# First layer of a graph network kernel: the sums and extrema of an entry made together in one PSUM bank, turned an iteration later and added at once, with a bank for each scan's transposes

## The chip, the cores and the metric

The kernel runs on one core of one Trainium2 chip. The metric is the device time of one execution in microseconds. A core has TensorE (PE, with its weight loads PEld), VectorE (DVE), ScalarE (ACT), GpSimd (POOL) and SyncE (SP), each with an instruction stream of its own; they meet through semaphores. Transfers are issued from SP, ACT and POOL queues and run on 16 DMA engines. TensorE's results go to PSUM, which has eight banks of 128 x 512 f32.

## The reference, cut to what matters

The program is a two-layer graph network over 6250 nodes and 206250 edges (sorted by target `dst`), 128 features. The change touches the first layer's edge stage alone. For each edge

```
z2 = concatenate([node_feat[src], node_feat[dst], edge_feat])
e = relu(z2 @ W_pre + b_pre)
deg = segment_sum(ones, dst)
s = segment_sum(e, dst)
mean_sq = segment_sum(e * e, dst) / safe_deg
mx = segment_max(e, dst)
mn = segment_min(e, dst)
```

that is: a message `e` for each edge, and per target node its count, sum, sum of squares, maximum and minimum. What follows (means, standard deviation, two dense layers, layer norms, a GCN and a GAT layer) is as it was.

## The kernel before, in words

`build` (L100) first makes tables in DRAM: `Atab` and `Btab`, the node features already multiplied by the source part and the target part of `W_pre`; masks `MM` that mark where a target's run of edges begins; and a list of **entries**. An entry is a chunk of 512 edges with a base node; its targets lie in a window of W = 64 nodes from the base. The list has T entries (read from `tb`), and every engine loops over it.

`phase_l0` (L443) is the first layer's edge stage. Each engine runs `pipeline(e, T, U, D, stages)` (L64) with U = 4 and D = 8: in iteration n it performs the listed steps in the written order, each for entry n minus its lag. Nothing else orders the work. `j.at(n)` (L47) is the entry's number plus n, so that `wait(e, s, j.at(-3))` waits until the step that raises `s` has been done for entry j-4, and `j.at(-1)` for entry j-2; `j.slot(4)` is the buffer number modulo 4. The loops are:

- **SyncE** (L513), `(0, loads), (2, load_dst)`. `loads` (L520) reads the entry's chunk and base from `tb`, waits for the gathers of j-4 and issues `ms` (source numbers, L529); waits for `p1` of j-4 and issues `ZR[0:64]` (edge features, 128 KB, L532) and `WB[64:128]` (64 rows of `Btab`, L533); waits for `d1` of j-4 and issues `dstb` (the targets of 512 edges on 64 partitions, 128 KB, L536). `load_dst` (L538) issues `md` (4 KB, L544).
- **GpSimd** (L548): four indirect gathers of `Atab` rows into `G` (L559).
- **VectorE** (L564), `(4, base), (2, d2), (0, d1), (2, hot), (4, d4a), (6, d4b), (4, d3)`. `d1` (L572) turns `dstb` into a one-hot of the target in `ZR[64:128]` (L577). `d2` (L580) adds `Z` and the gathered rows into `EE` (L585). `hot` (L588) makes one-hots `oh` of targets on edges' partitions (L593). `d4a` and `d4b` (L616 to L628) add turned results from the PSUM bank `TT` into `acc` (both at L622). `d3` (L598) runs the two scans, a running maximum and minimum over each target's run (L606, L608).
- **ScalarE** (L632), `(5, a2a), (1, masks), (2, a1), (5, a2b), (2, half), (3, e1), (5, e2)`. `a1` makes relu and square of an entry into `EE` (L639, L641), `half` a bf16 copy of four one-hots (L648), `masks` issues the mask transfer (L656), `a2a` and `a2b` copy the transposed scans from the bank `BK` to `BS` (L663), `e1` and `e2` copy sums (bank `S1`, L675) and extrema (bank `S2`, L681) to SBUF.
- **TensorE** (L685), `(5, p3a), (6, t2), (4, t1), (1, p1), (5, p3b), (3, p2), (5, p4)`. `p1` (L694) multiplies the 128 rows of `ZR` (64 edge features, 64 one-hot rows) with `WB` into `Z` (L702): the edge part plus the target part. `p2` (L706) transposes the relu'd messages into `ET` (L713) and makes sums and sums of squares with the one-hots into `S1` (L720). `t1` (L723) makes the counts (L732) and turns the sums (L733) into `TT`; `t2` (L736) turns the extrema (L740). `p3a` and `p3b` (L742 to L759) transpose the two scans one after the other through the one bank `BK` (L752), the second waiting for ScalarE's copy of the first. `p4` (L761) picks each target's last scan value with one-hots into `S2` (L769). `warm` (L691) is a matmul of zeros that is overwritten; it stands before the first group of `BK`, `Z` and `ET`.

All eight PSUM banks are in use (`Z` 2, `ET` 2, `S1`, `S2`, `BK`, `TT`). Slots before: `ms`, `md`, `ZR`, `WB`, `dstb`, `mm2`, `G`, `oh` four, `EE`, `ohb`, `ST`, `BS` two.

## Time and profile before

| | |
|---|---|
| median of 3 runs | 5884.95 us (5878.37 to 5885.05) |
| the profiled execution | 5883.57 us, its span 5881.6 us |
| mean granted TensorE clock | 0.95 of full |
| PE, DVE, POOL, ACT busy over the span | 92%, 82%, 67%, 48% |
| first layer's edge stage | from about 135 us to 2260 us |
| transfers over the span | 544.72 MB, mean 93 GB/s |

Busy shares are a mean over stages with different limits, so the stage is read by itself: a window gives busy time by engine, a group of lines the mean of one instruction, the waits what ended an engine's idle time, and the timeline the order of starts. Matmuls are pipelined and their ends are modelled, so distances from start to start are surer than durations on PE. A row "L622 ... x2" in a timeline is two instructions merged.

### The profile page before, as it was taken

What the parts mean: (1) busy time and instruction counts of PE and PEld (TensorE: products, weight loads), DVE (VectorE), ACT (ScalarE), POOL (GpSimd) and SP (SyncE); (2) the same over time, 40 slices, a digit from 0 to 9 for tenths busy, and PEclk for the clock granted to TensorE, in tenths of its full rate; (3) what the DMA queues carried; (4) which work ended last, traced back from release to release, by engine and by line L of the source; (5) the groups of instructions that cost most, each with busy time, mean ns of one, the idle gap of its engine ahead of it and who ended that gap; (6) DMA issues with size and microseconds to landing.
All of it is one profiled execution on the core that took longest, in us unless ns stands there. A gap on an engine that the chain in (4) does not pass through costs nothing. (4 is left out here: it accounts for less than half of the span.)

```text
span 5881.6 us, 179579 instructions
## 1 busy us (share of the span) xinstructions
PE 5388.7 (92%) x43454; PEld 4199.9 (71%) x44114; DVE 4796.1 (82%) x12693; ACT 2838.9 (48%) x6715; POOL 3926.1 (67%) x3976
## 2 busy tenths in 40 slices
PE   3999999999999997778888858999999999999993
PEld 3888888888888885457777735666666666666663
DVE  4999999999999996777777667777777777777777
ACT  1566666666666663133333244444444444444445
POOL 2777777777777772067777707777777777777762
PEclk7999999999999998878989869999999999999996
DMA  6666666666666663322222212222222222222221
GB/s 155 161 159 158 158 157 158 157 158 157 158 156 158 157 157 95 91 54 54 53 54 54 52 27 53 52 52 51 50 51 51 51 51 50 51 50 51 51 45 47
DMA packets 667245, 544.72 MB, mean 93 GB/s; under 512 B 365794, under 2 KB 544171, under 8 KB 666853
## 3 DMA queue, kind: packets, MB, share of 16 engines
q0 software_dynamic: 126336, 262.13, 18.9%
q1 hardware_dynamic: 415050, 163.69, 12.1%
q10 hardware_dynamic: 125724, 117.57, 7.7%
q14 instruction: 108, 0.88, 0.1%
q8 instruction: 27, 0.44, 0.0%
HBM read 517.22 MB, written 25.61 MB: 92 GB/s over the span
## 5 line engine op out<-in xcount | busy, mean ns | idle before, releaser
L1766 POOL DMA_INDIRECT Gt<-TAB,metat x1632 | 1631.9, 1000 | 705.9 <-issue 538.8
L559 POOL DMA_INDIRECT G<-Atab,ms x1616 | 1580.3, 978 | 572.3 <-issue 469.4
L1256 POOL DMA_INDIRECT Gc<-XS,metac x672 | 647.5, 964 | 240.1 <-issue 188.4
L1912 ACT COPY P<-PT 128x512 f32<-128x512 f32 x408 | 238.7, 585 | 805.7 <-PE PT L1956 739.0
L663 ACT COPY BS<-BK 128x512 f32<-128x512 f32 x808 | 465.6, 576 | 198.7 <-PE BK L752 190.4
L1401 ACT COPY acc<-CP 128x300 f32<-128x300 f32 x630 | 269.5, 428 | 557.2 <-PE CP L1439 552.3
L606 DVE TENSOR_TENSOR_SCAN ST<-mm,ST,ET 128x512 f32<-128x512 bf16 x404 | 516.7, 1279 | 0.2
L608 DVE TENSOR_TENSOR_SCAN ST<-mm,ST,ET 128x512 f32<-128x512 bf16 x404 | 506.9, 1255 | 0.0
L702 PE MATMUL Z<-WB,ZR 128*128 128x128 f32 x3232 | 429.3, 276 | 68.0 <-DVE ZR L577 67.7
L752 PE MATMUL BK<-ident,ST 128*128 128x128 f32 x3232 | 485.2, 273 | 2.4 <-ACT BS L663 1.8
L1970 PE MATMUL SR<-P,Gt 128*128 128x128 f32 x3264 | 472.8, 288 | 0.0
L1970 PEld LDWEIGHTS SR<-P,Gt 128*128 128x128 f32 x3264 | 395.0, 191 | 70.0 <-issue 70.0
L720 PE MATMUL S<-EE,oh 128*64 128x128 f32 x6464 | 442.2, 279 | 0.0
L1838 DVE TENSOR_TENSOR ln<-acc,LT 1x128 f32<-1x128 f32 x408 | 112.4, 275 | 400.5 <-PE LT L1940 385.9
L702 PEld LDWEIGHTS Z<-WB,ZR 128*128 128x128 f32 x3232 | 428.5, 193 | 11.9
L1414 PE MATMUL OT<-acc 128*128 128x180 f32 x2100 | 429.9, 331 | 0.5 <-ACT acc L1401 0.5
L769 PE MATMUL S<-BS,oh 128*64 128x128 f32 x6464 | 421.7, 273 | 1.4 <-issue 1.4
L639 ACT ACTIVATE EE<-EE 128x512 f32<-128x512 f32 x404 | 255.0, 631 | 347.2 <-issue 273.0
L1923 PE MATMUL SR<-zm,zw 128*128 128x512 bf16 x1531 | 413.6, 380 | 6.5 <-ACT P L1912 1.2
L752 PEld LDWEIGHTS BK<-ident,ST 128*128 128x128 f32 x3232 | 392.6, 141 | 32.8 <-issue 2.5
L1327 DVE TENSOR_SCALAR O<-iotaD,VA 128x300 bf16<-128x300 f16 x1260 | 400.9, 322 | 1.2
L720 PEld LDWEIGHTS S<-EE,oh 128*64 128x64 f32 x6464 | 344.7, 137 | 67.7 <-issue 67.7
(291 smaller groups left out, 12145.1 us busy)
## 6 DMA issues: line engine op xcount, KB each, us to landing
mm<-MM ACTq DMA_DIRECT2D x404, 256.0 KB
ZR<-in_eft SPq DMA_DIRECT2D x404, 128.0 KB
dstb<-DF SPq DMA_DIRECT2D x404, 128.0 KB
Gt<-TAB,metat POOLq DMA_INDIRECT x1632
G<-Atab,ms POOLq DMA_INDIRECT x1616
ad<-ADT SPq DMA_DIRECT2D x816, 0.2 KB
WB<-Btab SPq DMA_DIRECT2D x404, 32.0 KB
Gc<-XS,metac POOLq DMA_INDIRECT x672
```

The costliest lines, as they stand in the source:

```text
L559: e.indirect_dma_start(G[:, k, s, :], None, Atab, bass.IndirectOffsetOnAxis(ap=ms[:, k, s:s + 1], axis=0)).then_inc(l_g[k], 16)
L606: e.tensor_tensor_scan(ST[:, q, 0, :], mm2[:, k, 0, :], ET[q][:, :], ST[:, 1 - q, 0, CH - 1:CH], ALU.mult, ALU.max)
L608: e.tensor_tensor_scan(ST[:, q, 1, :], mm2[:, k, 1, :], ET[q][:, :], ST[:, 1 - q, 1, CH - 1:CH], ALU.max, ALU.min).then_inc(s_d3, 1)
L663: e.copy(BS[:, q, a, :], BK[:, :]).then_inc(s_a2[a], 1)
L702: mm = e.matmul(Z[q][:, s * 128:(s + 1) * 128], ZR[:, k, s * 128:(s + 1) * 128], WB[:, k, :], start=True, stop=True)
L720: mm = e.matmul(S1[a * 64:(a + 1) * 64, 0:128], oh[:, k, s, :], EE[:, q, a, s * 128:(s + 1) * 128], start=(s == 0), stop=(s == 3))
L752: mm = e.transpose(BK[:, s * 128:(s + 1) * 128], ST[:, q, a, s * 128:(s + 1) * 128], ident[:, :])
L769: mm = e.matmul(S2[a * 64:(a + 1) * 64, 0:128], oh[:, k, 4 + s, :], BS[:, q, a, s * 128:(s + 1) * 128], start=(s == 0), stop=(s == 3))
L1256: e.indirect_dma_start(G[:, k, s, :], None, XS, bass.IndirectOffsetOnAxis(ap=meta[:, k, s:s + 1], axis=0)).then_inc(l_g[k], 16)
L1414: mm = e.matmul(OT[k][:, 0:DB], acc[:, 0, h * 128:(h + 1) * 128], C[k][:, h, :], start=(h == 0), stop=(h == NB - 1))
L1766: e.indirect_dma_start(G[:, k, s, :], None, TAB, bass.IndirectOffsetOnAxis(ap=meta[:, k, s:s + 1], axis=0)).then_inc(l_g[k], 16)
L1970: m = e.matmul(SR[q][:, 0:2 * W], G[:, k, s, 0:128], P[:, q, s * 128:(s + 1) * 128], start=(s == 0), stop=(s == 3))
```

## The change

- The sums (`S1`) are no longer made in `p2` but in `p4`, beside the extrema, into one bank `S` (columns 0 to 127 and 128 to 255), and ScalarE copies both at once (`sums`) into `SN` of 256 columns.
- `t1` and `t2` become one step `across`, lag 6: counts, then both turns, into five adjacent parts of `TT`; `d4a` and `d4b` become one add `d4` of 5 x 64 columns, lag 7.
- The bank set free makes `BK` two banks, one for each scan. `p3a` and `p3b` now stand together and each waits only for the copy of its own bank an entry earlier.
- `EE` and `ohb` get four slots instead of two, so `d2` waits for `p4` of j-4 instead of `p2` of j-2.
- `WB` and `dstb` get two slots instead of four. `loads` waits for `p1` of j-2 before `ZR` and `WB`; `dstb` is issued by a step of its own, `load_col`, after a wait for `d1` of j-2.
- The tile of zeros `zm` goes; `warm` streams the 128 columns of `zw` four times.
- The orders on TensorE and ScalarE change as the diff shows.

The diff, without declarations of semaphores and unchanged lines:

```diff
-        WB = sbt(ph, "WB", [128, 4, 128])
-        dstb = sbt(ph, "dstb", [128, 4, CH])
+        WB = sbt(ph, "WB", [128, 2, 128])
+        dstb = sbt(ph, "dstb", [128, 2, CH])
-        EE = sbt(ph, "EE", [128, 2, 2, CH])
+        EE = sbt(ph, "EE", [128, 4, 2, CH])
-        ohb = sbt(ph, "ohb", [128, 2, 4, W], BF16)
+        ohb = sbt(ph, "ohb", [128, 4, 4, W], BF16)
-        S1 = pst(ph, "S1", [128, 512])
-        S2 = pst(ph, "S2", [128, 512])
-        BK = pst(ph, "BK", [128, CH])
+        S = pst(ph, "S", [128, 512])
+        BK = [pst(ph, f"BK{a}", [128, CH]) for a in range(2)]
...
             def loads(j):
-                gathered, done = 64 * j.uses(4, -1), j.at(-3)
+                gathered = 64 * j.uses(4, -1)
                 if not j.first(4):
                     wait_sync(e, l_g[k], gathered, s_sync)
                 e.dma_start(ms[:, k, :], src[0]).then_inc(l_ms[k], 16)
-                if not j.first(4):
-                    wait_sync(e, s_p1, done, s_sync)
+                if not j.first(2):
+                    wait_sync(e, s_p1, j.at(-1), s_sync)
                 e.dma_start(ZR[0:64, k, :], src[1]).then_inc(l_in[k], 16)
-                e.dma_start(WB[64:128, k, :], src[2]).then_inc(l_in[k], 16)
-                if not j.first(4):
-                    wait_sync(e, s_zr, done, s_sync)
-                e.dma_start(dstb[64:128, k, :], src[3]).then_inc(l_db[k], 16)
+                e.dma_start(WB[64:128, j.slot(2), :], src[2]).then_inc(l_in[k], 16)
+
+            def load_col(j):
+                k = j.slot(2)
+                c = e.snap(regs[j.slot(4)], min_val=0, max_val=NCH - 1)
+                if not j.first(2):
+                    wait_sync(e, s_zr, j.at(-1), s_sync)
+                e.dma_start(dstb[64:128, k, :], DF[ds(c * CH, CH)].partition_broadcast(64)).then_inc(l_db[k], 16)
...
-            pipeline(e, T, U, D, [(0, loads), (2, load_dst)])
+            pipeline(e, T, U, D, [(0, loads), (0, load_col), (2, load_dst)])
...
             def d2(j):
                 wait(e, s_p1, j.at(1))
                 wait(e, l_g[j.slot(4)], 64 * j.uses(4))
-                if not j.first(2):
-                    wait(e, s_p2, j.at(-1))
+                if not j.first(4):
+                    wait(e, s_p4, j.at(-3))
...
             def hot(j):
                     wait(e, s_p4, j.at(-3))
+                    wait(e, s_a1, j.at(-3))
...
-            def d4(j, S, n, lo, s_in, s_out):
+            def d4(j):
                 b = kept(e, regs, j)
-                wait(e, s_in, j.at(1))
+                wait(e, s_t, j.at(1))
                 if not j.first(1):
-                    wait(e, s_out, j.at())
-                a = acc[:, lo:lo + n, ds(b, W)]
-                e.tensor_tensor(a, a, S, ALU.add).then_inc(s_out, 1)
+                    wait(e, s_d4, j.at())
+                a = acc[:, 0:5, ds(b, W)]
+                e.tensor_tensor(a, a, TT[:, 0:5 * W].rearrange("p (a n) -> p a n", a=5), ALU.add).then_inc(s_d4, 1)
-            pipeline(e, T, U, D, [(4, base), (2, d2), (0, d1), (2, hot), (4, d4a), (6, d4b), (4, d3)])
+            pipeline(e, T, U, D, [(4, base), (2, d2), (0, d1), (2, hot), (7, d4), (4, d3)])
...
+            def sums(j):
                 wait(e, s_p4, j.at(1))
                 if not j.first(1):
-                    wait(e, s_t2, j.at())
-                e.copy(SN2[:, :], S2[:, 0:128]).then_inc(s_e2, 1)
-            pipeline(e, T, U, D, [(5, a2a), (1, masks), (2, a1), (5, a2b), (2, half), (3, e1), (5, e2)])
+                    wait(e, s_t, j.at())
+                e.copy(SN[:, :], S[:, 0:256]).then_inc(s_e, 1)
+            pipeline(e, T, U, D, [(5, a2a), (5, a2b), (2, a1), (1, masks), (3, half), (5, sums)])
...
             def warm(bank):
-                e.matmul(bank[:, :], zw[:, :], zm[:, :], start=True, stop=True)
+                e.matmul(bank[:, :], zw[:, :], zw[:, :].unsqueeze(1).to_broadcast([128, 4, 128]), start=True, stop=True)
...
+            def across(j):
+                wait(e, s_a1, j.at(1))
+                wait(e, s_e, j.at(1))
                 if not j.first(1):
-                    wait(e, s_e1, j.at())
+                    wait(e, s_d4, j.at())
                 for s in range(4):
-                    for a in range(2):
-                        mm = e.matmul(S1[a * 64:(a + 1) * 64, 0:128], oh[:, k, s, :], EE[:, q, a, s * 128:(s + 1) * 128],
-                                      start=(s == 0), stop=(s == 3))
-                mm.then_inc(s_p2, 1)
+                    e.matmul(TT[:, 2 * W:3 * W], onesb[:, :], ohb[:, j.slot(4), s, :], start=(s == 0), stop=(s == 3))
+                e.transpose(TT[:, 0:2 * W], SN[:, 0:128], ident[:, :])
+                e.transpose(TT[:, 3 * W:5 * W], SN[:, 128:256], ident[:, :]).then_inc(s_t, 1)
...
             def p3(j, a):
                 wait(e, s_d3, j.at(1))
-                if a == 1:
-                    wait(e, s_a2[0], j.at(1))
-                elif not j.first(1):
-                    wait(e, s_a2[1], j.at())
+                if not j.first(1):
+                    wait(e, s_a2[a], j.at())
...
             def p4(j):
+                wait(e, s_oh, j.at(1))
                 for a in range(2):
                     wait(e, s_a2[a], j.at(1))
                 if not j.first(1):
-                    wait(e, s_e2, j.at())
+                    wait(e, s_e, j.at())
                 for s in range(4):
                     for a in range(2):
-                        mm = e.matmul(S2[a * 64:(a + 1) * 64, 0:128], oh[:, k, 4 + s, :], BS[:, q, a, s * 128:(s + 1) * 128],
+                        e.matmul(S[a * 64:(a + 1) * 64, 0:128], oh[:, k, s, :], EE[:, k, a, s * 128:(s + 1) * 128],
+                                 start=(s == 0), stop=(s == 3))
+                for s in range(4):
+                    for a in range(2):
+                        mm = e.matmul(S[a * 64:(a + 1) * 64, 128:256], oh[:, k, 4 + s, :], BS[:, q, a, s * 128:(s + 1) * 128],
                                       start=(s == 0), stop=(s == 3))
                 mm.then_inc(s_p4, 1)
-            pipeline(e, T, U, D, [(5, p3a), (6, t2), (4, t1), (1, p1), (5, p3b), (3, p2), (5, p4)])
+            pipeline(e, T, U, D, [(5, p3a), (5, p3b), (1, p1), (3, p2), (6, across), (5, p4)])
```

## Rows read from the trace of the kernel before

**Rows 1.** The page, costliest groups: out<-in xcount, busy us, mean ns, idle before

```profile
L606 DVE TENSOR_TENSOR_SCAN ST<-mm,ST,ET 128x512 f32<-128x512 bf16 x404 | 516.7, 1279 | 0.2
```

**Rows 2.** Windows of the first layer: busy us per engine (count), granted clock, DMA share, GB/s

```profile
1000.00:2200.00 1200.00, 1188.11 (x13721) 1067.12 (x13949) 1135.81 (x1601) 721.62 (x1601) 889.15 (x913) 1.00 0.62 157
```

**Rows 3.** Groups of lines, 300 to 2150 us, columns as in group 1

```profile
L559 POOL DMA_INDIRECT G<-Atab,ms x1415 | 1383.8, 978 | 467.4 <-issue 410.4 <-DMA ms<-in_meta 43.9 <-DVE EE L585 13.1
L606 DVE TENSOR_TENSOR_SCAN ST<-mm,ST,ET 128x512 f32<-128x512 bf16 x353 | 451.5, 1279 | 0.2
```

**Rows 4.** Waits of VectorE, 404 to 2200 us: us in total, times, longest us

```profile
DVE EE L585 <- PE S L720: 31.6, 135, 0.5
```

**Rows 5.** Timeline of all engines, 1500 to 1511 us: start us, us, engine, line

```profile
1501.12 0.39 PE L692 MATMUL BK<-zm,zw 128*128 128x512 bf16 x1
...
1501.15 0.55 DVE L577 TENSOR_SCALAR ZR<-dstb,baseF,nid 64x512 f32<-64x512 f32 x1
...
1501.78 0.27 PE L740 MATMUL TT<-ident,SN 128*128 128x128 f32 x1
...
1502.20 0.39 PE L692 MATMUL Z<-zm,zw 128*128 128x512 bf16 x1
...
1502.43 1.05 PE L702 MATMUL Z<-WB,ZR 128*128 128x128 f32 x8
1502.45 0.58 DVE L622 TENSOR_TENSOR acc<-acc,TT 128x192 f32 x2
...
1504.22 1.25 DVE L608 TENSOR_TENSOR_SCAN ST<-mm,ST,ET 128x512 f32<-128x512 bf16 x1
1504.33 0.52 SPq L532 DMA_DIRECT2D ZR<-in_eft  x1
...
1504.50 1.09 PE L720 MATMUL S<-EE,oh 128*64 128x128 f32 x16
...
1505.71 0.47 SPq L536 DMA_DIRECT2D dstb<-DF  x1
...
1506.40 0.39 PE L692 MATMUL BK<-zm,zw 128*128 128x512 bf16 x1
```

**Rows 6.** Timeline, 1496.9 to 1499.2 us, where SyncE waited for the matmuls of p1

```profile
1497.14 1.06 PE L702 MATMUL Z<-WB,ZR 128*128 128x128 f32 x8
...
1498.43 0.50 SPq L532 DMA_DIRECT2D ZR<-in_eft  x1
```

**Rows 7.** Timeline of the stage's start, 140 to 165 us

```profile
139.69 0.54 SPq L536 DMA_DIRECT2D dstb<-DF  x1
139.88 1.91 PE L702 MATMUL Z<-WB,ZR 128*128 128x128 f32 x8
...
142.87 0.55 DVE L577 TENSOR_SCALAR ZR<-dstb,baseF,nid 64x512 f32<-64x512 f32 x1 [2.73 <-DMA dstb<-DF]
...
144.55 0.54 SPq L536 DMA_DIRECT2D dstb<-DF  x1
...
148.16 0.55 DVE L577 TENSOR_SCALAR ZR<-dstb,baseF,nid 64x512 f32<-64x512 f32 x1 [1.74 <-DMA dstb<-DF]
...
149.12 0.47 SPq L536 DMA_DIRECT2D dstb<-DF  x1
...
152.14 0.69 DVE L577 TENSOR_SCALAR ZR<-dstb,baseF,nid 64x512 f32<-64x512 f32 x1 [1.09 <-DMA dstb<-DF]
...
154.98 1.25 DVE L608 TENSOR_TENSOR_SCAN ST<-mm,ST,ET 128x512 f32<-128x512 bf16 x1
...
156.29 0.10 PEld L692 LDWEIGHTS BK<-zm,zw 128*128 128x128 bf16 x1 [0.87 <-DVE ST L608]
...
158.11 0.47 SPq L536 DMA_DIRECT2D dstb<-DF  x1
...
162.71 0.55 DVE L577 TENSOR_SCALAR ZR<-dstb,baseF,nid 64x512 f32<-64x512 f32 x1 [1.24 <-DMA dstb<-DF]
```

**Rows 8.** Window of the GCN stage, columns as in group 2

```profile
2500.00:3300.00 800.00, 685.40 (x4283) 569.85 (x4284) 586.88 (x2712) 255.59 (x600) 594.54 (x617) 0.87 0.22 54
```

More of the change, by code:

```diff
@@ L482, in phase_l0 @@
         l_in = [sem(f"l_in{k}") for k in range(4)]
-        l_db = [sem(f"l_db{k}") for k in range(4)]
+        l_db = [sem(f"l_db{k}") for k in range(2)]
         l_m = [sem(f"l_m{k}") for k in range(4)]
@@ L513, in _ @@
         def _(e):
-            for k in range(4):
+            for k in range(2):
                 e.dma_start(WB[0:64, k, :], d["wpre"][256:320, :]).then_inc(l_we, 16)
@@ L573, in d1 @@
                 k = j.slot(4)
-                wait(e, l_db[k], 16 * j.uses(4))
+                wait(e, l_db[j.slot(2)], 16 * j.uses(2))
                 if not j.first(4):
                     wait(e, s_p1, j.at(-3))
-                e.tensor_scalar(ZR[64:128, k, :], dstb[64:128, k, :], baseF[64:128, ds(j.at(), 1)], nid[64:128, 0:1],
+                e.tensor_scalar(ZR[64:128, k, :], dstb[64:128, j.slot(2), :], baseF[64:128, ds(j.at(), 1)], nid[64:128, 0:1],
                                 ALU.subtract, ALU.is_equal).then_inc(s_zr, 1)
@@ L643, in half @@
             def half(j):
-                q = j.slot(2)
+                q = j.slot(4)
                 wait(e, s_oh, j.at(1))
-                if not j.first(2):
-                    wait(e, s_t1, j.at(-1))
+                if not j.first(4):
+                    wait(e, s_t, j.at(-3))
                 e.copy(ohb[:, q, :, :], oh[:, j.slot(4), 0:4, :]).then_inc(s_a1, 1)
@@ L662, in back @@
                     wait(e, s_p4, j.at(-1))
-                e.copy(BS[:, q, a, :], BK[:, :]).then_inc(s_a2[a], 1)
+                e.copy(BS[:, q, a, :], BK[a][:, :]).then_inc(s_a2[a], 1)
             def a2a(j):
@@ L669, in a2b @@
                 back(j, 1)
[L671 to L677 removed]
+            def sums(j):
                 wait(e, s_p4, j.at(1))
                 if not j.first(1):
[L680 to L683 removed]
+                    wait(e, s_t, j.at())
+                e.copy(SN[:, :], S[:, 0:256]).then_inc(s_e, 1)
+            pipeline(e, T, U, D, [(5, a2a), (5, a2b), (2, a1), (1, masks), (3, half), (5, sums)])
         @blk.tensor
         def _(e):
[L687 to L688 removed]
+            e.wait_ge(l_we, 32)
+            e.wait_ge(s_i, 2)
             T = load_T(e, tb, 0)
             def warm(bank):
[L692 removed]
+                e.matmul(bank[:, :], zw[:, :], zw[:, :].unsqueeze(1).to_broadcast([128, 4, 128]), start=True, stop=True)
             def p1(j):
@@ L701, in p1 @@
                 for s in range(4):
-                    mm = e.matmul(Z[q][:, s * 128:(s + 1) * 128], ZR[:, k, s * 128:(s + 1) * 128], WB[:, k, :],
+                    mm = e.matmul(Z[q][:, s * 128:(s + 1) * 128], ZR[:, k, s * 128:(s + 1) * 128], WB[:, j.slot(2), :],
                                   start=True, stop=True)
@@ L712, in p2 @@
                 for s in range(4):
[L713 removed]
+                    mm = e.transpose(ET[q][:, s * 128:(s + 1) * 128], EE[:, j.slot(4), 0, s * 128:(s + 1) * 128], ident[:, :])
                 mm.then_inc(s_p2t, 1)
[L715 removed]
+            def across(j):
+                wait(e, s_a1, j.at(1))
+                wait(e, s_e, j.at(1))
                 if not j.first(1):
[L717 removed]
+                    wait(e, s_d4, j.at())
                 for s in range(4):
[L719 to L740 removed]
+                    e.matmul(TT[:, 2 * W:3 * W], onesb[:, :], ohb[:, j.slot(4), s, :], start=(s == 0), stop=(s == 3))
+                e.transpose(TT[:, 0:2 * W], SN[:, 0:128], ident[:, :])
+                e.transpose(TT[:, 3 * W:5 * W], SN[:, 128:256], ident[:, :]).then_inc(s_t, 1)
             def p3(j, a):
```

61 lines of the change are left out of this document (11 added, 50 removed).

## The prediction

> **What bounds the kernel now.** I read the page first, to find the stage the diff touches: the first layer handles 404 entries, one scan pair each [rows 1]. Windows inside that stage say which engine is full. TensorE is busy 99% of the time at its full granted clock, which is the 2.4 GHz level, VectorE 95%, and the transfers hold 62% of the DMA engines [rows 2]. The groups of lines over 1850 us give the pace: 353 scans, so one entry every 5.24 us, and GpSimd's four gathers at 0.98 us with 0.29 us of issue between them need 5.1 us of it [rows 3]. Then the waits. TensorE has none in the stage. VectorE waits for TensorE's sums of an entry two before, because `EE` has two slots: 31.6 us over 1796 us, or 0.09 us an entry [rows 4]. SyncE holds back `ZR` until the matmuls of `p1` end, and is let go at once [rows 6]. So TensorE's own sequence bounds, and VectorE, GpSimd and SyncE stand within about 5% of it. Such a kernel has little to win from a shorter wait and much to lose from a longer one.
>
> **The loop that the change closes.** Every engine runs its steps in the written order, and in iteration n a step with lag L works on entry n-L. `loads` now waits for `s_p1` at `j.at(-1)`, so the transfers for entry n are issued after the matmuls `p1(n-2)`, where before it was `p1(n-4)`. This follows from `WB` and `dstb` having two slots. `ZR` keeps four but stands behind the same wait, and `dstb` is issued third. In VectorE's iteration n stand `d2(n-2)`, `d1(n)`, `hot(n-2)`, the add, and the scans `d3(n-4)`. In TensorE's iteration n+1 stand first `p3a(n-4)` and `p3b(n-4)`, which wait for those scans, and then `p1(n)`. So `p1(n-2)` releases `dstb(n)`, that releases `d1(n)`, the scans behind `d1(n)` release TensorE, and `p1(n)` ends the loop. It advances two entries, so twice the period is at least its length:
> - From the start of `d1` to the end of the second scan: 1501.15 to 1504.22 + 1.25 = 1505.47, which is 4.32 us [rows 5]. The two adds in it, 0.58 us together [rows 5], become one over the same 320 columns. It lies between 0.29 us, half the pair, and 0.58 us; I take 0.52 us, near the pair, because the columns stay and only one start is saved: 4.26 us.
> - From the scan's end to TensorE: where TensorE waited for a scan it began at 156.29, the scan having ended at 154.98 + 1.25 = 156.23: 0.06 us [rows 7].
> - From the warming matmul of `BK` to the end of `p1`: 1501.12 to 1502.43 + 1.05 = 1503.48, 2.36 us. In it the turns of the sums (1501.78 to 1502.20, 0.42 us) give way to `p3b`'s four transposes. Four transposes with a warming matmul took 1501.12 to 1501.78, 0.66 us, and a warming matmul alone 0.23 us (1502.20 to 1502.43), so `p3b` takes 0.43 us [rows 5]: 2.37 us.
> - From the end of `p1` to the issue of `ZR` where SyncE waited for it: 1497.14 + 1.06 = 1498.20 to 1498.43, 0.23 us [rows 6].
> - From there to the issue of `dstb`: 1504.33 to 1505.71, 1.38 us, `WB` standing between [rows 5].
> - From that issue until `d1` runs. In the steady stage no row shows it, since `d1` never waits there. The nearest rows are those at the start of the stage, where it did: 139.69 to 142.87, 144.55 to 148.16, 149.12 to 152.14 and 158.11 to 162.71, so 3.18, 3.61, 3.02 and 4.60 us [rows 7]. I take their mean, 3.60 us, because the last one was issued among nearly the full traffic and the others among less, and keep 3.02 and 4.60 us as ends.
>
> All but the last is 4.26 + 0.06 + 2.37 + 0.23 + 1.38 = 8.30 us. With 3.60 us the loop is 11.90 us, the period 5.95 us. That is 0.71 us above 5.24 us, and 404 times it 287 us. Against the profiled execution's 5883.6 us this gives 6171 us; the median of the runs lies 1.4 us higher, which makes 6172 us. The ends give periods of 5.66 and 6.45 us, hence 6053 and 6372 us.
>
> The rule nearest to this: the Trainium skill, DMA: Bandwidth & Descriptors, section on the anatomy of one DMA, puts a transfer at about 2.0 us fixed plus bytes over 436 GB/s. An estimate from that page for the 128 KB of `dstb` is 2.3 us, with which the period would be 5.30 us and the time about 5908 us. None of the four rows is that short; what such a landing would do is rival 2.
>
> **The other parts.**
> - SyncE's own work: with nothing to wait for it issued `dstb` at 144.55 and 149.12, 4.57 us apart [rows 7]. Even with another 0.4 us of waits passed and loop turns it keeps 1.0 us of the 5.95 us free, so it stands ready when `p1` ends. Queued behind its longer wait are `md`, issued next after `dstb` and needed by `hot` right behind `d1`, and `ms` for the next gathers. `md` is 4 KB against 128 KB, so I cost it at nothing; if it landed last it could put up to 0.3 us into the loop, inside the ends above. GpSimd needs 5.1 us of 5.95 us and its rows of an entry are wanted two iterations later, so a later `ms` costs nothing while the period is above 5.1 us.
> - Single turn and single add: `across(n-6)` needs the add of entry n-7, which VectorE makes behind the late `d1(n)`. That path is d1's start to the add's end 1.82 us, 0.06 us, the six matmuls 0.4 us, then both groups of sums until the next iteration (1504.50 to 1506.40, 1.90 us [rows 5]): 4.2 us, against 4.32 us by the scans. It is the next limit, 0.1 us behind, and costs nothing of its own. In the profile TensorE's idle time may be shown half before `across`.
> - Sums made two iterations later, `EE` and `ohb` in four slots: VectorE's wait for them (0.09 us) goes. It is not a saving, since `d1` is what comes last now.
> - `BK` in two banks: `p3b` no longer waits for ScalarE's copy. TensorE had no such wait, so nothing. The same copies, one 256-column copy for two of 128, leave ScalarE near the 60% it shows now [rows 2].
> - The warming matmul reads one block four times in place of `zm`. The plain one costs 0.39 us (0.23 us to the next start) [rows 5]. I take the same; were it twice as slow, the two of them in the loop would add 0.46 us, 0.23 us a period, 93 us in all. Less than now is excluded, as the columns streamed are the same.
> - One lag more (7) lengthens the end by part of one iteration, under 3 us: nothing beside the sum.
>
> **The rivals.**
> 1. The transfer lands early enough, and TensorE still bounds. It decides at 2 x 5.24 - 8.30, a landing of 2.2 us. Then the order counts: turns and row counts made at once save part of the 0.42 us [rows 5], by perhaps 0.09 us an entry, and VectorE's slack no longer matters: 404 x 0.09 = 36 us, so 5848 us, **faster**. For it: 99% busy [rows 2], and that transfers started with a lighter load. Against: the shortest landing seen is 0.8 us too long. 7%.
> 2. The landing is shorter than any row shows, between 2.2 and 2.4 us, and the loop just touches TensorE's pace. The period is then 5.25 to 5.35 us, and if the reorder gives nothing back the time is 5888 to 5928 us. For it: the landings at the start spread over 1.6 us, so they hang on what else is moving, and a slower stage moves less. Against: the shortest of the four is 3.02 us, and three of them came while fewer transfers moved than in the steady stage. 6%, of which 4% within 0.2% and 2% above. This is the case of the page's figure named above.
> 3. The clock falls too. TensorE would be idle 0.75 us of 5.95 us. The GCN stage shows what can come with gaps: 685 us busy of 800 us at a granted 0.87 [rows 8], which is 26% of the time at the 1.2 GHz level. There `p1` took 1.91 us [rows 7] against 1.05 us [rows 5], so a TensorE iteration of 5.2 us becomes 9.5 us. With 26% of the time at it the period is 1 / (0.74 / 5.95 + 0.26 / 9.5) = 6.6 us, and the time about 6430 us. For it: `p3a`, `p3b` and their warming matmul now stand together, a long stretch of transposes. Against: the gap is short, and the same three warming matmuls stay in each iteration. 7%. The Trainium skill, TensorE: Matmul & The Clock Gate, Part 4 on transposes, says that transposes do not count as busy in the way matmuls do, which speaks for this case; no row here separates it.
>
> **How the numbers follow.** The loop as costed has 80%, so 6172 us. Its ends are 6053 and 6372 us; I round them outward to 6050 and 6380 us. That leaves out the first two rivals (13%) and the clock case (7%). A measurement can tell this kernel from no change by about 0.2%, 12 us. Slower: 80 + 7 + 2 = 89%; within 0.2%: 4%; faster: 7%.
>
> **What would show it.** Right: a period near 5.95 us; `d1` waiting about 1 us in each entry for the `dstb` transfer; TensorE about 87% busy in the stage, idle before `BK`'s warming matmul or before the row counts; SyncE waiting long for `p1`; VectorE's wait for the sums gone; the later stages unchanged. Wrong: no DMA wait at `d1` and TensorE still 99% busy (rival 1 or 2), or a granted clock under 1.0 (rival 3). A wait of `hot` on `md`, or of the gathers on `ms`, would mean that the loop was closed at another place.

## The result and the profile after

The kernel after takes 6742.1 us (median of 3 runs, 6720.04 to 6742.46) against 5884.95 us: 1.145 times as long, interval 1.1411 to 1.1485. The forecast was 6172 us, with a range to 6380 us: the direction was right, the size was not, and the time lies above the range.

Three quarters of the loss, 637.7 of 859 us, are in the first layer, where the forecast put all of the loss; the rest is where it put nothing. First the page of the kernel after; q14 is the queue that brings the engines their instructions:

```profile
q14 instruction: 361, 2.96, 0.1%
...
L554 POOL DMA_INDIRECT G<-Atab,ms x1616 | 1547.0, 957 | 1250.6 <-DMA ms<-in_meta 781.6
...
L571 DVE TENSOR_SCALAR ZR<-dstb,baseF,nid 64x512 f32<-64x512 f32 x404 | 225.6, 558 | 539.0 <-DMA dstb<-DF 527.7
...
L601 DVE TENSOR_TENSOR_SCAN ST<-mm,ST,ET 128x512 f32<-128x512 bf16 x404 | 514.5, 1274 | 0.0
```

`d1` (L571) stood idle 527.7 us for `dstb`, 1.3 us an entry, which the forecast named as the sign of its loop. The last line answers to [rows 1]. q14 moved 361 packets of instructions; the page of the kernel before has 108 there, which becomes the key to the second part of the loss.

How long the first layer is, from the first to the last start of a scan, in the view of one source line (minimum, median and maximum in ns, then those two starts in us), before and after:

```profile
L606 DVE TENSOR_TENSOR_SCAN ST<-mm,ST,ET x404: 1267/1279/1282, 153.8 to 2268.4; 128x512 f32<-128x512 bf16 x135
```

```profile
L601 DVE TENSOR_TENSOR_SCAN ST<-mm,ST,ET x404: 1267/1273/1278, 152.3 to 2904.6; 128x512 f32<-128x512 bf16 x135
```

2114.6 us became 2752.3 us, that is 5.25 us an entry became 6.83 us (403 steps): 637.7 us. From the last scan to the end of the span 3613.2 us (5881.6 - 2268.4) became 3836.0 us (6740.6 - 2904.6): 222.8 us in stages whose code the change doesn't touch.

Windows of the kernel after, of the scan of L601 alone (us, busy us, times, granted clock, DMA share, GB/s), and the whole row of one of them:

```profile
404.00:1000.00 596.00, 115.19 (x91) 0.96 0.49 126
1000.00:2200.00 1200.00, 225.79 (x178) 0.93 0.47 122
2200.00:2850.00 650.00, 110.79 (x88) 0.87 0.44 110
```

```profile
1000.00:2200.00 1200.00, 1011.32 (x10803) 886.44 (x10803) 842.80 (x1063) 532.68 (x1062) 678.12 (x710) 0.93 0.47 122
```

Against [rows 2] TensorE is busy 84% instead of 99%, and the clock is no longer 1.00 throughout: a granted 0.93 is about 14% of the time at the 1.2 GHz level. An entry takes 596 / 91 = 6.55 us at a granted 0.96, 1200 / 178 = 6.74 us at 0.93, and 650 / 88 = 7.39 us at 0.87. The pace falls with the clock, but it is far above 5.24 us even where the clock is nearly full.

The waits of the kernel after, 300 to 2150 us (us in total, times, longest):

```profile
POOL G L554 <- DMA ms<-in_meta: 467.5, 150, 5.2
DVE ZR L571 <- DMA dstb<-DF: 327.5, 165, 4.8
...
PE TT L705 <- DVE acc L617: 276.4, 146, 4.6
```

And a timeline of two entries at full clock, every step of the forecast loop in it:

```profile
1501.29 0.39 PE L675 MATMUL BK<-zw 128*128 128x512 bf16 x1
...
1502.61 1.05 PE L685 MATMUL Z<-WB,ZR 128*128 128x128 f32 x8
...
1503.89 0.48 SPq L523 DMA_DIRECT2D ZR<-in_eft  x1
...
1505.43 0.40 SPq L531 DMA_DIRECT2D dstb<-DF  x1
...
1506.51 0.39 PE L675 MATMUL BK<-zw 128*128 128x512 bf16 x1
...
1510.08 0.55 DVE L571 TENSOR_SCALAR ZR<-dstb,baseF,nid 64x512 f32<-64x512 f32 x1 [2.69 <-DMA dstb<-DF]
...
1511.73 1.27 DVE L601 TENSOR_TENSOR_SCAN ST<-mm,ST,ET 128x512 f32<-128x512 bf16 x1
...
1511.96 0.28 PE L705 MATMUL TT<-ohb,onesb 128*128 128x64 bf16 x4 [2.43 <-DVE acc L617]
...
1512.92 1.25 DVE L603 TENSOR_TENSOR_SCAN ST<-mm,ST,ET 128x512 f32<-128x512 bf16 x1
...
1514.32 0.39 PE L675 MATMUL BK<-zw 128*128 128x512 bf16 x1
...
1515.64 1.05 PE L685 MATMUL Z<-WB,ZR 128*128 128x128 f32 x8
```

The steps follow one another as predicted: `p1` ends at 1502.61 + 1.05 = 1503.66; `ZR` is issued 0.23 us later, `dstb` 1.54 us after it; `d1` runs 4.65 us after that issue, having stood idle 2.69 us for it; its scans end at 1514.17, TensorE restarts 0.15 us later and ends `p1` at 1516.69. That is 13.03 us for two entries, in one short turn (1501.29 to 1506.51, 5.22 us) and one long (7.81 us). TensorE's idle time is shown before `across`, at L705, as the forecast said it might be.

One thing about the runs below: in some jobs the kernel before itself took 7820 to 7870 us instead of 5885 us, all runs of the job alike, so every ratio there is to the kernel before of the same job.

### The profile page after: what moved, and what is told of

Read it like the earlier page. It is cut to its first block and busy times, and to the rows that moved or that the text cites. A ratio compares the mean times of both kernels' runs of the same rounds, so it can differ in the third digit from the quotient of the medians.

```text
span 6740.6 us, 178054 instructions
## 1 busy us (share of the span) xinstructions
PE 5686.3 (84%) x43859; PEld 4377.8 (65%) x44114; DVE 4711.0 (70%) x12288; ACT 2782.4 (41%) x6311; POOL 3880.2 (58%) x3976
## 5 line engine op out<-in xcount | busy, mean ns | idle before, releaser
L571 DVE TENSOR_SCALAR ZR<-dstb,baseF,nid 64x512 f32<-64x512 f32 x404 | 225.6, 558 | 539.0 <-DMA dstb<-DF 527.7
L664 ACT COPY SN<-S 128x256 f32<-128x256 f32 x404 | 150.4, 372 | 1080.1 <-PE S L739 1019.6
L735 PE MATMUL S<-EE,oh 128*64 128x128 f32 x6464 | 514.0, 309 | 1.1 <-ACT BS L652 1.1
L601 DVE TENSOR_TENSOR_SCAN ST<-mm,ST,ET 128x512 f32<-128x512 bf16 x404 | 514.5, 1274 | 0.0
L579 DVE TENSOR_TENSOR EE<-Z,G 128x512 f32<-128x512 f32 x404 | 279.4, 691 | 307.0 <-PE S L739 292.2
L705 PE MATMUL TT<-ohb,onesb 128*128 128x64 bf16 x1616 | 116.3, 196 | 446.8 <-DVE acc L617 434.6
L739 PE MATMUL S<-BS,oh 128*64 128x128 f32 x6464 | 491.7, 302 | 0.0
L1893 PE MATMUL SR<-zm,zw 128*128 128x512 bf16 x1531 | 448.1, 405 | 6.5 <-ACT P L1882 1.2
L735 PEld LDWEIGHTS S<-EE,oh 128*64 128x64 f32 x6464 | 401.7, 153 | 76.1 <-issue 76.1
L739 PEld LDWEIGHTS S<-BS,oh 128*64 128x64 f32 x6464 | 437.3, 157 | 0.0
L1829 DVE TENSOR_TENSOR acc<-acc,SR 128x128 f32 (+1 forms) x816 | 232.1, 284 | 283.5 <-issue 221.9
```

The costliest lines, as they stand in the source:

```text
L579: e.tensor_tensor(EE[:, j.slot(4), 1, :], Z[j.slot(2)][:, :], G[:, j.slot(4), :, :].rearrange("p s f -> p (s f)"), ALU.add).then_inc(s_d2, 1)
L601: e.tensor_tensor_scan(ST[:, q, 0, :], mm2[:, k, 0, :], ET[q][:, :], ST[:, 1 - q, 0, CH - 1:CH], ALU.mult, ALU.max)
L735: e.matmul(S[a * 64:(a + 1) * 64, 0:128], oh[:, k, s, :], EE[:, k, a, s * 128:(s + 1) * 128], start=(s == 0), stop=(s == 3))
L739: mm = e.matmul(S[a * 64:(a + 1) * 64, 128:256], oh[:, k, 4 + s, :], BS[:, q, a, s * 128:(s + 1) * 128], start=(s == 0), stop=(s == 3))
L1893: e.matmul(bank[:, :], zw[:, :], zm[:, :], start=True, stop=True)
```

## The experiments

The expectations on record speak of "the last scan of the first layer" and "the rest". The scan meant there is VectorE's last of the program, that over the degrees, which stands 22 to 28 us behind the last message scan; the starts given here are of the message scan.

### Where the kernel before takes 5885 us

| kernel | ratio to before, interval | first to last scan, us | span behind it, us | q14 packets |
|---|---|---|---|---|
| before | 1 | 153.8 to 2268.4 | 3613.2 | 108 |
| after | 1.1448 [1.1411, 1.1485] | 152.3 to 2904.6 | 3836.0 | 361 |
| e11, `ms` ahead | 1.1444 [1.1397, 1.1492] | 152.8 to 2894.9 | 3837.8 | 361 |
| e16, `dstb` ahead of the wait, padded | 1.0374 [1.0357, 1.0391] | 153.2 to 2473.4 | 3614.6 | 108 |
| e10, wait three back | 1.0359 [1.0341, 1.0376] | 151.4 to 2250.3 | 3833.2 | 361 |
| e17, wait three back, padded | 0.9987 [0.9978, 0.9996] | 154.8 to 2254.8 | 3622.4 | 108 |

**e16: dstb's load ahead of the wait, and 55 idle instructions on VectorE.** The kernel after with

```diff
 e.dma_start(ms[:, k, :], src[0]).then_inc(l_ms[k], 16)
+if not j.first(2):
+    wait_sync(e, s_zr, j.at(-1), s_sync)
+e.dma_start(dstb[64:128, kc, :], DF[...]).then_inc(l_db[kc], 16)
 if not j.first(2):
     wait_sync(e, s_p1, j.at(-1), s_sync)
...
-pipeline(e, T, U, D, [(0, loads), (0, load_col), (2, load_dst)])
+pipeline(e, T, U, D, [(0, loads), (2, load_dst)])
...
 pipeline(e, T, U, D, [(4, base), (2, d2), (0, d1), (2, hot), (7, d4), (4, d3)])
+for _ in range(55):
+    e.engine_nop()
```

> The kernel after with dstb's load issued before the wait for TensorE's last pass, and with 55 idle instructions on VectorE behind its first-layer loop. If the chip runs the kernel before in about 5885 us: placement theory, 108 instruction packets and 3590 to 3600 us after the first layer's last scan (rival: 361 or no gain, 3810 us); loop theory with dstb's landing as its largest term, the last scan at 2290 to 2530 us (it was 2931 us), so a ratio of 1.00 to 1.04; rival (other transfers behind the wait cost as much), last scan above 2750 us, ratio 1.08 or more. If the chip is one that needs 7840 us for it: first layer about 3630 to 3680 us, the rest about 4470 us, ratio 1.035 to 1.045, which tells nothing new of dstb.

Measured: 6099.06 us. The first layer is 432 us shorter than in the kernel after (2320.2 us, 5.76 us an entry) and the rest 221 us. The two edits act in different stretches of time: one changes SyncE's order in the first layer, the other stands behind VectorE's work there. So both causes are there, apart from each other. Its waits, and a stretch of its timeline:

```profile
POOL G L551 <- DMA ms<-in_meta: 159.9, 92, 3.4
DVE oh L585 <- DMA md<-MD: 130.4, 130, 3.2
PE TT L704 <- DVE acc L614: 90.9, 111, 3.0
```

```profile
1000.00:2200.00 1200.00, 1107.21 (x12635) 963.76 (x12633) 991.34 (x1243) 623.03 (x1242) 793.27 (x829) 1.00 0.55 142
```

```profile
1499.73 0.72 PE L684 MATMUL Z<-WB,ZR 128*128 128x128 f32 x5
...
1500.61 0.47 SPq L527 DMA_DIRECT2D ZR<-in_eft  x1
...
1502.14 0.34 SPq L536 DMA_DIRECT2D md<-MD  x1
...
1503.30 0.39 PE L674 MATMUL BK<-zw 128*128 128x512 bf16 x1
...
1504.62 1.05 PE L684 MATMUL Z<-WB,ZR 128*128 128x128 f32 x8
...
1505.57 0.75 DVE L585 SCALAR_TENSOR_TENSOR oh<-iotaW,baseF,md 128x512 f32<-128x512 f32 x1 [0.81 <-DMA md<-MD]
...
1507.83 1.25 DVE L600 TENSOR_TENSOR_SCAN ST<-mm,ST,ET 128x512 f32<-128x512 bf16 x1
...
1509.22 0.39 PE L674 MATMUL BK<-zw 128*128 128x512 bf16 x1
...
1510.54 1.05 PE L684 MATMUL Z<-WB,ZR 128*128 128x128 f32 x8
```

`d1` no longer waits for a transfer, the clock is back at 1.00, and still the pace is not 5.24 us. `hot` (L585) now waits for `md`: that is the next load that `hot` needs from behind the same wait. `p1` ends at 1499.73 + 0.72 = 1500.45; `ZR` at 1500.61, `md` at 1502.14, `hot` 3.43 us later at 1505.57, the scans' end at 1507.83 + 1.25 = 1509.08, `BK` at 1509.22, `p1`'s end at 1511.59. From end to end of `p1` that is 11.14 us for two entries, or 5.57 us each (5.76 us measured over the stage). The range on record for the last scan (2290 to 2530 us) held; that the loop's largest term was all of it did not. No run moved `md` alone, and the gathers still wait for `ms` too, so `md` is the next limit by this timeline and not by an experiment.

**e10: the wait three entries back.** First came e1, below, whose slots it has: `WB` and the loaded row in four slots each, the row loaded into `ZR` itself and turned in place, and the wait four back. Then

```diff
 if not j.first(4):
-    wait_sync(e, s_p1, j.at(-3), s_sync)
+    wait_sync(e, s_p1, j.at(-2), s_sync)
```

> The four-slot kernel with the wait on TensorE's last pass put three entries back (it was four back; two back in the kernel after). Loop theory: a loop of about 13 us, closed over three entries, allows 4.3 us an entry, which does not bind; the first layer's last scan ends near 3300 to 3350 us, as with four back, and the ratio to the kernel before is 1.01 to 1.02. Rival (every step that the wait comes nearer costs something, since SyncE's queue holds other transfers behind it): the last scan ends between, near 3400 to 3500 us, ratio 1.025 to 1.04. At two back it was 3616 us and 1.0525.

Measured: 6095.88 us. The first layer takes 2098.9 us, 5.21 us an entry, so all of the loss in it is gone and 16 us more. The expected ratio and last scan came from jobs of the other kind (below) and missed: the rest still had its 220 us.

```profile
1000.00:2200.00 1200.00, 1200.00 (x14024) 1074.53 (x14020) 1092.68 (x1381) 692.84 (x1380) 919.78 (x920) 1.00 0.63 158
```

TensorE is busy without a break, at full clock, and SyncE waits for `p1` 48.4 us in these 1200 us where it waits 295.3 us in the kernel after. e11, next, has the same slots and the near wait, and its first layer takes 2742.1 us. `j.at(-2)` against `j.at(-1)` is thus the whole of the first layer's loss: a loop of some 13 us closed over three entries allows 4.3 us, over two 6.5 us, and TensorE's pace of 5.2 us lies between. The single add, the joint turns and the banks, which e10 keeps, cost nothing.

**e11: ms in a step of its own, an entry ahead of the near wait.**

```diff
-pipeline(e, T, U, D, [(0, loads), (0, load_col), (2, load_dst)])
+pipeline(e, T, U, D, [(0, load_src), (1, loads), (1, load_col), (3, load_dst)])
```

It is e9's kernel (below) otherwise: four slots, the wait two back.

> The four-slot kernel with the wait two entries back, but the loads of the source indices (ms), which feed GpSimd's gathers, are issued one entry earlier by a step of their own, so that they no longer stand behind that wait on SyncE. Theory that the near wait costs through the late indices and so late gathers: GpSimd's waits for ms vanish and the last scan of the first layer ends at 3400 us or sooner, ratio at most 1.025. Rival, that it costs through dstb's own load and turn (ZR, targets) alone: GpSimd's waits for ms vanish too, but the last scan still ends near 3600 us and the ratio stays near 1.05.

Measured: as the kernel after, 1.1444. The gathers' waits for `ms` did not vanish (267.4 us over 1200 us, where the kernel after has 318.6 us): `ms`, now one entry ahead, still stands in SyncE's one queue behind the wait for `p1`, so the edit doesn't separate what it was made to separate. What it does show is that four slots bring nothing where the wait stays near (2742.1 us).

**e17: e10 with 60 idle instructions on VectorE behind its first-layer loop** (e12's kernel once more).

> The kernel of e12 once more (four slots, wait three entries back, 60 idle instructions on VectorE). On a chip that runs the kernel before in about 5885 us: 108 packets, first layer's last scan near 2277 us, the rest 3590 to 3600 us, 5870 to 5885 us in all, ratio 0.997 to 1.000; rival, a ratio of 1.03 or more if the padding brings nothing here. On a chip that needs 7840 us: as e12, ratio near 1.003.

Measured: 5879.31 us, 0.9987 times the kernel before of the same job, interval 0.9978 to 0.9996. Padding alone takes the rest from 3833.2 to 3622.4 us. Their first layers end within 5 us of each other, so one window of the GAT stage shows why. VectorE's waits at 4200 to 5000 us, in e10:

```profile
DVE acc L1826 <- issue: 68.5, 34, 2.3
```

and the packets of instructions in that window, e10 (the kernel before and e17 have no such line):

```profile
q14 instruction: 84, 0.69, 0.3%
```

and the windows themselves, e10, then e17:

```profile
4200.00:5000.00 800.00, 753.39 (x4353) 499.34 (x4436) 576.68 (x1880) 360.01 (x942) 533.63 (x539) 0.96 0.23 47
```

```profile
4200.00:5000.00 800.00, 795.15 (x4795) 534.52 (x4888) 634.79 (x2074) 392.96 (x1037) 595.77 (x592) 1.00 0.25 51
```

TensorE gets through 4353 matmuls in e10 and 4795 in e17, 10% more. In the kernel after the stall comes once each turn of VectorE's loop, which is 8 entries or some 47 us:

```profile
5019.04 0.58 DVE L1829 TENSOR_TENSOR acc<-acc,SR 128x128 f32 x2 [4.81 <-issue]
...
5066.68 0.58 DVE L1829 TENSOR_TENSOR acc<-acc,SR 128x128 f32 x2 [4.68 <-issue]
```

All waits "issue" at this line of the kernel after, and at the same line of the kernel before (L1859 there), us in total and times:

```profile
  issue: 221.9, 49
```

```profile
  issue: 0.2, 1
```

That is the 222.8 us. And q14 in one such stall, 5014.00 to 5019.04 us of the kernel after:

```profile
q14 instruction: 2, 0.02, 0.9%
```

In the trace's records each of the 49 stalls, 4.1 to 4.8 us long, has an instruction packet within 0.2 us of its start and another 2.3 to 3.0 us into it; the kernel before has none from 3650 to 5700 us. So VectorE waits for its own code. The padding was chosen by the author's count, 403 different instructions of VectorE in the first layer of the kernel before and 348 in that of the kernel after. The trace's records from the first `d1` to the scan over the degrees, each turn of the loop counted once, give 278 and 232, so the code behind moves up by some 50 instructions. 55 or 60 that do nothing bring it near enough to its old place; how near it has to be was not tested. The Trainium skill, Runtime: NRT & Kernel Launch, section on instruction fetch mechanics, says that code is fetched in blocks of 256 instructions of which two are held, and that a taken branch out of them waits for a fetch. The trace agrees, in that packets and stalls come and go together with where the loop lies (49 stalls and 361 packets, or none and 108); no run here shows the block size itself.

### Where the kernel before takes 7820 to 7870 us

It is not the chip: the one that ran e7, e8 and e9 in such a job ran e10, e11 and e17 beside a kernel before at 5885 us. The first layer of the kernel before, unedited, there takes 3164.4 us (b0; 162.8 to 3327.2 us). VectorE and ScalarE wait for a release that no record of the profile stands for:

```profile
ACT SN L675 <- remote: 410.4, 116, 4.2
DVE EE L585 <- remote: 312.6, 117, 4.2
```

```profile
1000.00:2200.00 1200.00, 916.67 (x9211) 784.29 (x9365) 743.37 (x1076) 477.15 (x1074) 647.24 (x615) 0.92 0.40 106
```

TensorE is busy 917 us of 1200 us at a granted 0.92, so it has slack there that it lacks in the other jobs, and VectorE and ScalarE wait for the sums without a record of what held them. Why was not settled. The runs of these jobs tell less apart: a near wait costs 308 to 425 us there too (e9 against e1, e2 against b0), but not by `dstb` being late. e0 was expected at 1.05 to 1.145 and came at 1.0654; b0's scan over the degrees was expected near 3320 us and came at 3350 us. Where a kernel ran twice, its last scan moved by 16 to 47 us (e7 and e13, e2 and e15, e3 and e14), so smaller differences in this table mean nothing.

| run | edit | ratio, interval | last scan, us | q14 |
|---|---|---|---|---|
| b0 | before, unedited | one run | 3327.2 | 108 |
| e0 | after, unedited | 1.0654 [1.0591, 1.0717] | 3655.6 | 361 |
| e1 | after, four slots, wait four back | 1.0166 [1.0112, 1.022] | 3281.0 | 361 |
| e2 | before, two slots, wait two back | 1.0496 [1.0454, 1.0538] | 3752.0 | 108 |
| e3 | after, `dstb` ahead of the wait | 1.0621 [1.0575, 1.0666] | 3609.4 | 361 |
| e4 | after, `dstb` first behind the wait | 1.0483 [1.0423, 1.0544] | 3568.5 | 361 |
| e5 | after, three warming matmuls in `p2` | 1.0605 [1.0536, 1.0673] | 3625.2 | 361 |
| e7 | after, 55 idle instructions | 1.0416 [1.038, 1.0453] | 3638.4 | 108 |
| e8 | e1, 60 idle instructions | 0.9958 [0.9939, 0.9977] | 3289.0 | 108 |
| e9 | e1, wait two back | 1.0525 [1.0477, 1.0573] | 3589.3 | 361 |
| e12 | e10, 60 idle instructions | 1.003 [1.0012, 1.0048] | 3323.9 | 108 |
| e13 | e7 once more | 1.0439 [1.0397, 1.048] | 3654.9 | 108 |
| e14 | e3 once more | 1.0575 [1.0541, 1.0609] | 3656.2 | 361 |
| e15 | e2 once more | 1.0522 [1.0489, 1.0555] | 3729.2 | 108 |

**e1 and e9.** e1 undoes the two slots:

```diff
-WB = sbt(ph, "WB", [128, 2, 128])
-dstb = sbt(ph, "dstb", [128, 2, CH])
+WB = sbt(ph, "WB", [128, 4, 128])
...
-if not j.first(2):
-    wait_sync(e, s_p1, j.at(-1), s_sync)
+if not j.first(4):
+    wait_sync(e, s_p1, j.at(-3), s_sync)
...
-e.dma_start(dstb[64:128, k, :], DF[...].partition_broadcast(64)).then_inc(l_db[k], 16)
+e.dma_start(ZR[64:128, k, :], DF[...].partition_broadcast(64)).then_inc(l_db[k], 16)
```

and e9 is e1 with the wait at `j.at(-1)` again.

> Everything of the change stays except the two slots: WB has four again, and the targets' rows are loaded straight into ZR[64:128] (four slots, d1 works in place), so that all transfers of an entry wait for p1 of four entries before, as in the kernel before. Theory A (the loop p1(n-2) -> transfers -> d1(n) -> scans -> p1(n) is the whole loss, and the clock falls only because TensorE idles in it): no DMA wait at d1, granted clock 1.00, period back to 5.15 to 5.30 us, time 5850 to 5910 us. Rival B (the single turn and add, the sums made two iterations later, or the new orders cost by themselves): waits of TensorE for the add or of d2 for p4 stay at 0.5 us an entry or more, time above 6100 us.

> The version with four slots, and one number changed: the wait for p1 before the transfers of an entry is again for two entries before instead of four. The buffers stay as in that version, so this is the wait's distance alone. Theory A: the loss of the first layer comes back whole, its last scan moves from 3307 us to 3600 to 3780 us and the ratio to 1.055 to 1.075. Rival (the separate dstb tile, its own step or its wait cost): it stays under 3400 us.

The last scan comes 375 us earlier with e1 (3655.6 to 3281.0), and e9 loses 308 of them again. The slots by themselves are worth little, the wait's place nearly all.

**e2: the kernel before with two slots and the near wait**, `dstb` in a step of its own as in the change, and nothing else of it.

```diff
-WB = sbt(ph, "WB", [128, 4, 128])
-dstb = sbt(ph, "dstb", [128, 4, CH])
+WB = sbt(ph, "WB", [128, 2, 128])
+dstb = sbt(ph, "dstb", [128, 2, CH])
...
-    wait_sync(e, s_p1, done, s_sync)
+    wait_sync(e, s_p1, j.at(-1), s_sync)
```

> The kernel before with this one part of the change: WB and dstb in two slots, the p1 wait at j-2, dstb issued by a step of its own. Theory A: the same loop closes in the old order, since p1 still stands behind the first scan's transposes: the loop without low clock 12.7 us as in the changed kernel, so a period of 6.3 to 6.9 us and a time of 6320 to 6750 us, with d1 waiting for the dstb transfer. Rival B (the loss needs the new orders too): under 6150 us.

These make the last scan 425 us later than b0's, with the old order of the other work.

**e3, e4, e5: a term of the loop each.** e3 is e16 without the padding (it ran first). e4 issues `dstb` first behind the wait. e5 has

```diff
-                warm(ET[q])
+                for _ in range(3):
+                    warm(ET[q])
```

> The changed kernel with the dstb transfer issued before the wait for p1(n-2), behind its own wait for d1(n-2) alone; slots and everything else as changed. Theory A: this opens the loop, since ZR and WB of an entry are wanted an iteration later than dstb: d1 hardly waits, clock back near 1.00, period 5.2 to 5.4 us, 5860 to 5960 us. Rival B: above 6300 us. If md (issued behind ZR and WB) closes the same loop through hot, the wait moves to hot and the time lies between, 6100 to 6500 us.

> The changed kernel with the order of the transfers behind the p1(n-2) wait turned: dstb first, then ZR and WB. Only the place of dstb in the loop changes, by the 1.47 us that ZR and WB now take ahead of it. Theory A: the two-entry loop falls from 12.7 to 11.3 us, the period at full clock from 6.36 to 5.65 us; with the clock low for a few per cent less of the time than now the whole comes to 6050 to 6350 us. Rival (the loop does not go through the issue of dstb): no change beyond 1%, 6700 to 6800 us.

> The changed kernel with two more warming matmuls in p2 (three for each group of ET, each 0.22 us of TensorE, in the place where it waits anyway before the row counts). In the changed kernel the clock is at its lower level for 14% of the first layer. Theory A (the low clock costs 0.5 us an entry by itself: 12.7 us for two entries without it, 13.7 us on the mean): with the clock held up the period falls from 6.86 to 6.4 us, 150 to 200 us less than the changed kernel. Rival (the clock falls only where TensorE waits anyway and costs nothing): within 1% of the changed kernel, or slower by the added matmuls (up to 0.2 us an entry, 80 us). The share of time at the lower level in the first layer is read from the granted clock of its windows.

All three missed: the last scan comes 46, 87 and 30 us earlier than e0's. The 46 us went in e14, the same kernel as e3 (3656.2 us against 3655.6 us), so only e4's 87 us may be a gain. `d1`'s waits for `dstb` were few already (e0: 22.3 us over the 1200 us of the window, against 214.6 us in the kernel after). In e5 the granted clock of the window rose to 0.92 from e0's 0.90, and the pace did not follow. For the regime of the forecast e16 gives the answer that e3 could not.

**e7 and e8: VectorE's code.** 55 idle instructions behind the loop of the kernel after, 60 behind e1's.

> The changed kernel with 55 empty instructions on VectorE behind its first-layer loop. VectorE executes 403 different instructions in the first layer before the change and 348 after it, so the padding puts all later VectorE code back where it was. Theory C (the 220 us that the first comparison lost behind the first layer come from where the GAT loop's code now lies: VectorE stops once in each turn of that loop for 4.6 us while code is fetched): instruction packets on q14 fall from 361 to about 108, the time behind the last scan from 4683 us to about 4500 us, 150 to 200 us less in all, with the first layer unchanged at about 3680 us. Rival (later stages lose by transfers or by the clock): no change beyond 0.5%, q14 still 361.

> Both repairs: four slots for the transfers (targets loaded into ZR itself) and 60 empty instructions on VectorE, 343 to 403. By theories A and C together nothing of the loss is left: ratio to the kernel before 0.990 to 1.002. If the rest of the change gains as its order suggests (TensorE's waits gone), below 0.995.

Both as expected: 361 packets became 108, behind the last scan e7 takes 4515 us where e0 takes 4709 us, and e8 is the one kernel that is ahead of the kernel before there, by 0.4%. e12, with the wait three back instead of four, does not: 1.003.

> The kernel of e10 (four slots, wait three entries back: 6095.88 us, first layer's last scan 2277 us, 3807 us after it, 361 instruction packets) with 60 idle instructions on VectorE behind its first-layer loop. Theory of code placement: packets fall to 108 as in the kernel before, the rest falls from 3807 to about 3590 to 3600 us, and the kernel takes 5870 to 5885 us, ratio to before 0.997 to 1.000. Rival (the 217 us outside the first layer come from something else that the first layer leaves behind): the rest stays near 3800 us and the ratio near 1.036.

e13, e14 and e15 are the kernels of e7, e3 and e2 again, with expectations for jobs of the other kind; their ratios agree with those of the first runs within 0.5%.

> The kernel after with 55 idle instructions on VectorE behind its first-layer loop, nothing else. Theory of code placement: the first layer stays as it is (last scan near 2930 us), the rest falls from 3810 to about 3590 us, the kernel takes 6510 to 6530 us, ratio near 1.108. Rival: both stay, 6740 us, 1.145.

> The kernel after with dstb's load issued before SyncE's wait for TensorE's last pass, everything else as it is. Loop theory of the prediction, with dstb's landing as its largest term (3.6 predicted, about 4.3 to 4.7 us seen): the wait of the first turn for dstb vanishes and what is left of the loop is ZR's own load, 2 us or more shorter over two entries, so the first layer gains 1.0 to 1.6 us an entry, its last scan ends at 2290 to 2530 us and the ratio falls to 1.04 to 1.08. Rival (the near wait costs by the other transfers queued behind it too: WB, Z's targets, the source indices): the wait for dstb vanishes but the last scan stays above 2750 us, ratio above 1.11.

> The kernel before with dstb and WB in two slots and SyncE's wait two entries back, so the near wait alone, with the old vector and tensor work. Theory (the near wait is the whole loss of the first layer, the loop closes over two entries): last scan of the first layer at 2850 us or later, the rest near 3590 us with 108 packets, ratio 1.09 or more. Rival (the loss needs the added scan transposes and adds in one bank too): last scan below 2500 us, ratio below 1.04.

None of the three falls under these numbers, since the regime was not theirs; only the packets did what e13's says, 361 to 108.

## Why the prediction was wrong

The mechanism, a loop over two entries closed by the near wait, was right; three terms of the sum were not. Of the 570 us between forecast and result, some 186 us are the landing in the loop, taken at 3.60 us where it was 4.44 us; some 165 us are the clock, left to a rival; and 222.8 us are the later stages, which the forecast called unchanged and which the moved code made slower.

- **The loop** held as built: `p1(n-2)`, `ZR`, `dstb`, `d1`, the scans, TensorE, `p1(n)`. Term by term, predicted and in the timeline above: `d1` to the scan's end 4.26, 4.09; to TensorE 0.06, 0.15; to `p1`'s end 2.37, 2.37; to `ZR`'s issue 0.23, 0.23; to `dstb`'s 1.38, 1.54. Together 8.30 and 8.38 us.
- **The first failed step is the landing**: "I take their mean, 3.60 us". It was 4.65 us there, and in the next turns in which `d1` waited 4.39, 4.70 and 4.02 us:

```profile
1518.40 0.49 SPq L531 DMA_DIRECT2D dstb<-DF  x1
...
1532.70 0.49 SPq L531 DMA_DIRECT2D dstb<-DF  x1
...
1545.72 0.49 SPq L531 DMA_DIRECT2D dstb<-DF  x1
```

```profile
1522.79 0.55 DVE L571 TENSOR_SCALAR ZR<-dstb,baseF,nid 64x512 f32<-64x512 f32 x1 [2.38 <-DMA dstb<-DF]
...
1537.40 0.55 DVE L571 TENSOR_SCALAR ZR<-dstb,baseF,nid 64x512 f32<-64x512 f32 x1 [2.66 <-DMA dstb<-DF]
...
1549.74 0.55 DVE L571 TENSOR_SCALAR ZR<-dstb,baseF,nid 64x512 f32<-64x512 f32 x1 [2.01 <-DMA dstb<-DF]
```

  The four average 4.44 us. In the trace's records of the last 384 entries `d1` stood idle over 0.5 us in 208, and there the median was 4.38 us, the mean 4.57 us. With 4.44 us the loop is 8.38 + 4.44 = 12.82 us and the period 6.41 us, so 404 times 1.17 us, 473 us instead of 287 us. The row at 4.60 us [rows 7] was the one issued into nearly full traffic, as the text itself says; the mean gave three lightly loaded landings the weight. The Trainium skill's 2.0 us and bytes over 436 GB/s (DMA: Bandwidth & Descriptors, anatomy of one DMA), 2.3 us for these bytes as an estimate, is a fit to transfers that GpSimd issues, while `dstb` is issued by SyncE. It is not what this load, behind others in a busy stage, takes from issue to use: the trace says 4.0 to 4.7 us.
- **The clock** was made a rival of 7%, with the loop otherwise as costed. It was no alternative to the loop but came with it. What is left of 637.7 us beyond 473 us, some 165 us, is an estimate of its share, and no run measured it apart; by the windows, with 6.55 us at 0.96 and 7.39 us at 0.87, a straight line to 1.00 gives 6.2 us, and so up to 250 us. Pairs of entries that lie wholly in time at the full level took 6.31 us an entry in the trace's records (112 pairs), which is between the two. The Trainium skill's sentence on transposes (TensorE: Matmul & The Clock Gate, Part 4) is neither shown nor refuted: in e16 the same instructions in the same order had 1.00 at 92% busy. e5 tried to hold the clock up only in a job of the other kind.
- **"the later stages unchanged"** failed by 222.8 us, a term that stood at nothing without a reason given. The forecast priced a stage's instructions and not where the code behind them comes to lie. e17 against e10 gives 211 us back with idle instructions alone, and e16 has 221 us less behind the first layer than the kernel after.
- **md**, "up to 0.3 us into the loop", "I cost it at nothing": right as long as `dstb` comes last, but in e16's timeline it is the next limit, with a period of 5.57 us, 0.8 us below the 6.41 us of `dstb`. The waits of the gathers for `ms` were priced at nothing too; e10 removes them (7.3 us left in the window) and the rest of the loss with one constant, so they come with the same wait, and their own price wasn't separated.
- **Right**: the add 0.48 us instead of two at 0.29 (0.52 taken), the warming matmul unchanged at 0.38 to 0.39 us, no gain from banks, slots of `EE` or the order. Rival 1's gain exists once the wait is back: 0.04 us an entry where 0.09 was allowed.
- The sum: 287 predicted; 473 loop, 165 clock, 223 code: 861, against 859 us of span (6740.6 - 5881.6). The first two are an estimated split of the measured 637.7 us, the third is measured.

## What to carry to other kernels

A wait for work d entries back costs nothing while the loop through it is shorter than d times the pace. The loop runs from the release over the issue, the landing and every engine in turn back to the release: here 13 us at a pace of 5.2 us needs three entries, and two cost 640 us. Price a landing in such a loop by the loaded rows, and look at what is queued behind it, since removing the first late transfer uncovers the next. When a change alters how many instructions an engine has, compare the instruction packets of both pages before explaining time in a stage that wasn't touched: a few idle instructions test it.

## What was not expected of the hardware

- VectorE's loop in a later stage lost 4.1 to 4.8 us a turn of some 47 us, and the kernel 211 to 223 us, from a shift of its code by some 50 instructions; packets of instructions 108 and 361. In the kernel after each stall begins with an instruction packet.
- The same kernel on the same chip took 5885 us in one job and 7867 us in another, with a mean granted clock of 0.896 in the longer (b0) and 0.950 in the profiled run of before. Within a job it was steady: 15 runs of the kernel before between 5883 and 5892 us beside e17. The cause stays open, and with it why there a near wait costs 308 to 425 us although `dstb` is rarely late.
